# Convolution sequence on one core: weights ahead of x at the head, one t2 half later in the first image, the last image's products reordered

## What is computed

```python
t1 = p1_w * x                          # per channel and row
t2 = x + t1
t4 = relu(x)
t7 = einsum('oc,chw->ohw', p7_w, t4)   # 128 x 128 product
t12 = mean over 5 taps (x - t7 shifted by 3 columns each)
t5 = unfold(x, 3 x 7)                  # 21 neighbours of each pixel
t10 = grouped 1x1 conv of t2 (4 groups, weights p10_w)
t11 = t1 @ t5^T / sqrt(4096)
t13 = t11 @ t10 / sqrt(128 * 21)
out = maximum(t13, t12)
```

## Time and profile before

| | us |
|---|---|
| median of 3 runs | 413.93 |
| lowest and highest run | 413.47, 414.99 |
| the profiled execution | 411.89 |
| its span (first to last instruction) | 409.9 |
| PE busy | 398.8 (97% of the span) |
| DVE busy | 333.6 (81%) |
| ACT busy | 249.4 (61%) |
| POOL busy | 90.0 (22%) |
| DMA queue 1 | 51.4% of 16 engines' span |

### The profile page before, as it was taken

The page is one execution under the profiler, slowest core; times in us unless marked ns, Lnnn a source line. Parts: engine busy times, 40 slices in busy tenths (PEclk is TensorE's granted clock), DMA queues, the critical chain, the costliest instruction groups (busy, mean ns, idle before and its releaser), DMA issues.

```text
span 409.9 us, 12373 instructions
## 1 busy us (share of the span) xinstructions
PE 398.8 (97%) x5126; PEld 250.5 (61%) x5126; DVE 333.6 (81%) x401; ACT 249.4 (61%) x714; POOL 90.0 (22%) x75
## 2 busy tenths in 40 slices
PE   7999999999999999999999999999999999999995
PEld 2333655668655586666888886444766668443663
DVE  6999968899788887888888887888868888786904
ACT  1336728777377755777277771777727775477970
POOL 0582200232023300332003320033202330033300
PEclk9999999999999999999999999999999999999999
DMA  8973263644665447663475635645455542632105
GB/s 295 406 304 109 86 238 116 210 162 158 206 197 176 151 140 221 191 224 104 169 241 201 203 117 187 232 164 164 163 209 187 169 157 80 216 128 95 54 28 206
DMA packets 24104, 72.40 MB, mean 177 GB/s; under 512 B 2800, under 2 KB 3056, under 8 KB 24048
## 3 DMA queue, kind: packets, MB, share of 16 engines
q1 hardware_dynamic: 24048, 71.61, 51.4%
HBM read 54.82 MB, written 16.78 MB: 175 GB/s over the span
## 4 chain that ended last, share of the span: by engine, by line
PE 84%; issue 6%; POOL 3%; DVE 3%; ACT 2%; DMA 2%; DVEq 0%; SPq 0%; ACTq 0%; POOLq 0%
PE ps_y L654 44%; PE ps_y L666 16%; PE ps_p L666 12%; PE ps_t L666 12%; POOL t1T L219 3%; DMA xw<-x_conv 2%; ACT t L314 1%; DVE v_planes L463 0%; DVE v_planes L440 0%; DVE yT L495 0%; DVE v_planes L449 0%; ACT base L259 0%; DVE base L538 0%; ACT relu_pad L272 0%; DVEq L43 0%
## 5 line engine op out<-in xcount | busy, mean ns | idle before, releaser
L654 PE MATMUL ps_y<-v_planes,u_planes 64*64 64x512 f32 x2048 | 257.0, 590 | 0.4
L654 PEld LDWEIGHTS ps_y<-v_planes,u_planes 64*64 64x64 f32 x2048 | 126.1, 133 | 93.6 <-issue 54.7
L219 POOL TENSOR_TENSOR t1T<-t1T,p1T_sb 128x512 f32<-128x512 f32 x64 | 84.1, 1340 | 281.4 <-DVE box L513 152.2
L314 ACT ACTIVATE t<-xn,p_plus 128x64 f32<-128x64 f32 x512 | 128.1, 335 | 0.0
L666 PE MATMUL ps_p<-box,p_fifth 64*64 64x512 f32 x464 | 123.4, 590 | 1.6 <-ACT ps_p L259 1.0
L666 PE MATMUL ps_t<-t,aT 64*64 64x512 f32 x448 | 118.4, 590 | 0.0
L259 ACT ACTIVATE base<-ps_p 128x512 f32<-128x512 f32 x58 | 34.6, 596 | 85.4 <-PE ps_p L666 85.4
L666 PEld LDWEIGHTS ps_y<-t1T,yT 64*64 64x64 f32 x2048 | 58.0, 133 | 8.4 <-DVE yT L495 5.0
L666 PE MATMUL ps_y<-t1T,yT 64*64 64x128 f32 x2048 | 60.7, 270 | 2.0 <-issue 1.2
L666 PEld LDWEIGHTS ps_p<-box,p_fifth 64*64 64x64 f32 x464 | 38.3, 133 | 22.7 <-issue 13.8
L482 DVE SCALAR_TENSOR_TENSOR ps_y<-ps_y,q_sb 128x512 f32<-128x512 f32 x32 | 22.3, 698 | 33.8 <-ACT q_sb L259 33.7
(11 more groups left out here) (42 smaller groups left out, 119.2 us busy)
## 6 DMA issues: line engine op xcount, KB each, us to landing
xw<-x_conv SPq DMA_DIRECT2D x32, 594.0 KB, 5.4
xn<-x_nat SPq DMA_DIRECT2D x32, 512.0 KB, 4.1
t1T<-x_pix SPq DMA_DIRECT2D x32, 512.0 KB, 6.1
out<-base SPq DMA_DIRECT2D x64, 256.0 KB, 2.5
u_planes<-w_tiles SPq DMA_DIRECT2D x4, 384.0 KB, 7.1
p1T_sb<-p1T SPq DMA_DIRECT2D x1, 128.0 KB, 7.5
p_sb<-p7T SPq DMA_DIRECT2D x1, 64.0 KB, 7.3
p_sb<-p SPq DMA_DIRECT2D x1, 32.0 KB, 7.8
```

The costliest lines, as they stand in the source:

```text
L219: nc.gpsimd.tensor_tensor(part, part, p1T_sb[:, e, :].unsqueeze(1).broadcast_to([P, 4, C]), ALU.mult).then_inc(t1_ready, 1)
L314: last = nc.scalar.activation(t2[:, h, W * r:W * (r + 1)], xn[:, f, at:at + W], ACT.Copy, scale=p1_plus[:, 8 * h + r:8 * h + r + 1])
L654: last = nc.tensor.matmul(dst[TILE * pair:TILE * pair + TILE, :], u_planes[rows, u % GROUPS, weights, TILE * k:TILE * k + TILE], v_planes[ ...
```

## The change

It makes no operation faster and leaves out none but part of one zero product. It reorders:

1. **Head.** SP issues the weights of a group ahead of its x for groups 0 and 1; DVE does `weights(0)` ahead of `early_planes(0)` and `weights(1)` ahead of `early_planes(1)`. The three zero products are now one of 256 columns on half of the p7 bank, then t13's bank, then p7's.
2. **First image.** ACT's list loses one t2 half ahead of `relu(1, 1)`; each later `t2_half` stands one place later until image 2's first half, where an extra one catches up.
3. **Around unit 31.** On PE, `outputs_second` of halves b moves behind the rest of unit 31 and `outputs_first` of c. On DVE `turn_y(31)` moves ahead of `max_half(6, 6)` and `box_pairs(7, 3)`.
4. **Last p7 products.** The groups between the blocks of `y_times_t1(7)` move from 16, 24 and 32 blocks to 22, 28 and 32, and each pairs a product of row half 0 with one of row half 1. On ACT `base_half(7, 3)` moves behind `t2_half(7, 3)`, `t2_half(7, 7)` behind `base_half(7, 5)`, and `first_part_of_a(7)` ahead of `base_half(7, 6)`.

```diff
+            load_weights(0)
             load_group(0)
-            load_weights(0)
+            load_weights(1)
             load_group(1)
-            load_weights(1)
...
                     t2_half(0, 4)
-                    t2_half(0, 5)
...
+                late = n == 1
                 relu(n, 1)
                 base_half(n - 1, 6)
                 seed_x(n - 1, 7)
-                t2_half(n - 1, 6)
+                t2_half(n - 1, 6 - late)
...
             seed_x(LAST, 5)
+            t2_half(LAST, 3)
             base_half(LAST, 3)
-            t2_half(LAST, 3)
             seed_x(LAST, 6)
             seed_x(LAST, 7)
-            t2_half(LAST, 4)
             base_half(LAST, 4)
-            for h in range(5, 8):
+            for h in range(4, 7):
                 t2_half(LAST, h)
             base_half(LAST, 5)
+            t2_half(LAST, 7)
+            first_part_of_a(LAST)
             base_half(LAST, 6)
-            first_part_of_a(LAST)
             base_half(LAST, 7)
...
+            weights(0)
             early_planes(0)
-            weights(0)
+            weights(1)
             early_planes(1)
-            weights(1)
             early_planes_rest()
...
             box_last(LAST, 2)
+            turn_y(UNITS - 1)
             max_half(LAST - 1, 6)
             box_pairs(LAST, 3)
-            turn_y(UNITS - 1)
             box_fours(LAST, 3)
...
-            for bank_set in (ps_t13, ps_p7, ps_p7):
-                nc.tensor.matmul(bank_set[:], zeros[:, 0:P], zeros[:, 0:HALF], start=True,
+            for bank_set in (ps_p7[:, 0:HALF // 2], ps_t13, ps_p7):
+                nc.tensor.matmul(bank_set[:], zeros[:, 0:P], zeros[:, 0:bank_set.shape[-1]], start=True,
...
             zero_three(UNITS - 1, False, 0)
-            outputs_second(p_b, t_b, done + 4)
             zero_three(UNITS - 1, False, 1)
             outputs_first(p_c, t_c, done + 5)
+            outputs_second(p_b, t_b, done + 4)
             outputs_second(p_c, t_c, done + 5)
 
-            y_times_t1(LAST, 0, BLOCKS)
-            p7_rows(LAST, 5, 0)
-            p7_rows(LAST, 6, 0).then_inc(item_half, 1)
-            y_times_t1(LAST, BLOCKS, BLOCKS + 8)
+            y_times_t1(LAST, 0, BLOCKS + 6)
+            p7_rows(LAST, 6, 0, True)
+            p7_rows(LAST, 5, 1, True).then_inc(item_half, 1)
+            y_times_t1(LAST, BLOCKS + 6, BLOCKS + 12)
             pe.wait_ge(item_half, done + 6)
-            p7_rows(LAST, 5, 1).then_inc(p7_done, 1)
-            p7_rows(LAST, 7, 0).then_inc(item_half, 1)
-            y_times_t1(LAST, BLOCKS + 8, 2 * BLOCKS)
+            p7_rows(LAST, 5, 0).then_inc(p7_done, 1)
+            p7_rows(LAST, 7, 1, True).then_inc(item_half, 1)
+            y_times_t1(LAST, BLOCKS + 12, 2 * BLOCKS)
             pe.wait_ge(item_half, done + 7)
             p7_rows(LAST, 6, 1).then_inc(p7_done, 1)
-            p7_rows(LAST, 7, 1).then_inc(p7_done, 1)
+            p7_rows(LAST, 7, 0).then_inc(p7_done, 1)
```

More of the change, by code:

```diff
@@ L360, in _ @@
                     t2_half(0, 4)
-                    t2_half(0, 5)
+                elif n == 2:
+                    relu(1, 3)
+                    base_half(1, 2)
+                    seed_x(1, 3)
+                    t2_half(1, 1)
+                    base_half(1, 3)
+                    seed_x(1, 4)
+                    copy_two(8)
+                    t2_half(1, 2)
+                    relu(2, 0)
+                    base_half(1, 4)
+                    seed_x(1, 5)
+                    t2_half(1, 3)
+                    first_part_of_a(1)
+                    t2_half(1, 4)
+                    base_half(1, 5)
+                    seed_x(1, 6)
+                    copy_two(9)
+                    t2_half(1, 5)
                 else:
@@ L388, in _ @@
                 copy_two(u + 2)
-                t2_half(n - 1, 7)
+                t2_half(n - 1, 7 - late)
                 relu(n, 2)
@@ L393, in _ @@
                 seed_x(n, 1)
-                t2_half(n, 0)
+                if late:
+                    t2_half(n - 1, 7)
+                else:
+                    t2_half(n, 0)
                 base_half(n, 1)
@@ L397, in _ @@
                 copy_two(u + 3)
-                t2_half(n, 1)
+                if late:
+                    t2_half(n, 0)
+                else:
+                    t2_half(n, 1)
             seed_x(LAST, 3)
@@ L731, in y_times_t1, with p7_rows @@
                     last.then_inc(a_done, 1)
-            def p7_rows(n, h, half):
-                if half == 0:
+            def p7_rows(n, h, half, first=False):
+                if first:
                     pe.wait_ge(box_steps, BOX_STEPS * (4 * n + h // 2 + 1))
@@ L757, in outputs_first @@
                     if n >= 0:
-                        last = p7_rows(n, h, 0)
+                        last = p7_rows(n, h, 0, True)
                 for n, h in (t,):
```

## The result

The changed kernel takes 408.80 us (median of six runs, 408.13 to 409.64) where the kernel before takes 413.74 (six runs, 412.67 to 414.99). The ratio is 0.989, with a 95% interval of 0.9872 to 0.9907.

A forecast was written before the change was run, and what follows sets the result against it. PE was taken as the bound, busy 398.8 of 409.9 us. Head -0.25, first image -1.31 and tail -1.54 sum to -3.10 us, from the median 413.93 to 410.8 us; range 409.4 to 412.5.

The forecast's parts named there:

- Direction and places: Whole kernel: faster (under 411.86 us, chance 0.68), by PE's idle time at the head, first image and tail.
- Head, -0.25: Kernel start: weights ahead of x and shorter zero products start PE's convolutions earlier; -0.25 us, ends -0.5 and +0.5.
- The fourth rival: Head: PE's clock rises later; some 3 us late +1.2 us (chance 0.09), over 7 us late slower (chance 0.03).
- First image, -1.31: First image: PE's wait for ACT's seed goes whole, as one t2 half leaves the relu's front; ends -1.3 and -0.9.
- DVE didn't take it back: First image, rival: DVE's full stretch from 73.6 doesn't start earlier, so the 1.31 us shrinks towards 0; 412.1 us, chance 0.10.
- Tail, -1.54: Unit 31 to the first t13: y starts 1.05 us earlier and t13 1.54 us earlier; ends 0.5 and 2.3.
- POOL's part: Around unit 31: POOL's last t1 part, 2.36 us beside DVE's pair sum, takes 1.27 once the sum comes later.
- ACT took the place of the removed wait: Tail: ACT's t2 half ahead of the A copy makes it start at 395.85, 1.5 us behind PE.
- (b): First image: moved t2 halves release x's buffers later; quarter 3's load of image 1 stays hidden, 5.5 us against 3.7 to 5.6.
- the seed's 1.3: First image: the 1.31 us PE loses waiting for ACT's seed, forecast to go whole.
- Theory A and C: Formed after the forecast. A: the first trace of before was lucky somewhere. C: loads delay PE's instruction fetches in y_times_t1.

The follow-up runs named there:

- e7: The changed kernel with ACT's first_part_of_a of the last image ahead of its t2 half 7: 406.92 us, ratio 0.9853 against the kernel before.
- e4: The kernel before, with only SP's load of image 2's x, quarter 1, and what queues behind it waiting one more t2 half: 411.77 us, ratio 0.9976.
- e2: The kernel before with the first image's part of the change alone, t2 half 5 one place later: 410.40 us, ratio 0.9933.
- e11: The changed kernel with ACT's A copy ahead of t2 half 7, and x's quarter 1 loaded one t2 half later in images 3 to 7: 404.69 us.
- e3: The kernel before with all of the tail's edits alone (unit 31's order, transposes, p7 groups, ACT's order): 411.71 us, ratio 0.996.

## Why the prediction was right or wrong

- **Direction and places**: right. PE is the bound, and each of the three places gave time.
- **Head, -0.25**: right as a mean. 0.3 was timed, within noise of about 1, and the traces give 0.25 where the rise isn't late. The 0.83 between the two first traces came about because x of unit 1 landed late in the first of before (8.0, in six others of the old order at 7.0 to 7.3) and x of both units early in that of after (5.3 and 8.1; 5.65 and 8.9 were forecast, and in other traces of the new order they were at 5.4 to 6.3 and 8.1 to 9.1). The fourth rival is real: it took place in 2 of 8 traces, at its short form. Its 0.5 us for each us is what the two spacings give (0.85 and 0.43), and a rise 4 us late cost some 1.6 us of PE. No run shows that PE's idle 0.7 us is the cause, nor a rise over 7 us late.
- **First image, -1.31**: the wait went in full, and DVE didn't take it back.
- **Tail, -1.54**: 1.64 by starts, 1.65 timed alone. POOL's part shrank to 1.27 as reasoned (the pair sum beside it had lost a little too, 1.58 against 1.32). Ahead of the result that was a guess from one overlap, in the trace of before; the 48 long parts of the 17 traces show it. ACT took the place of the removed wait: e7 got 1.5 us for that alone.
- **The step that failed** is the passage on the moved t2 halves under "First image" (b). It saw that the transfers behind them would be issued later, asked only whether they would come *too late*, and booked nothing. That they had been coming at a bad time before, into `y_times_t1(1)`, was overlooked. This is a term of -1.0 to -1.5: 1.0 for the load's move alone (e4), 1.5 left of e2's 2.8 beside the seed's 1.3, and 1.25 by the loops (7.05 and five times 8.3 to 9.3 in the six traces with the load at its old place, mean 8.55; 7.30 in both of the changed kernel).
- It could have been suspected. The prediction noted that the profiled execution was 2.04 us below the median and that "nothing in the trace tells of" it. The trace did hold a sign: the same loop took 7.05 to 8.01 us in different images, though all its work is the same. Theory A and C together account for both gaps: 3.8 by starts, less 1.1 lost by longer loops, is 2.7 where the spans show 2.8; and 0.3 (head) + 1.3 + 1.5 (first image) + 1.6 (tail) = 4.7 where the runs show 4.9.
- Without that term the sum was 3.1, and its parts held to 0.1 us. That a sum of starts from one execution came so close to the mean is in part luck, as the head's starts show.

## What to carry to other kernels

When the median of the runs lies well above the one traced execution, look for a place that varies before using that trace's terms: the same loop with unequal durations, or idle time put down to nothing. In this dense loop of short matmuls two fetches of instructions lie 3.5 us apart (e4); a bulk load issued just ahead of the loop held PE back by up to 2.1 us, and issuing that load a few microseconds later cost nothing that could be measured, as its user had slack. And when PE's order is changed around a unit's end, look whether the order of the engine that makes its operands must go with it (2.6 us here).

## What was unexpected of the hardware

- An instruction fetch of 16 KB came 2.9 us into the loop when DMA was 92% busy with data, against 0.4 us when it was idle; PE lost up to 2.1 us for one of them and always went on 1.1 to 1.6 us after its packet. Five loops gained about 0.4 us each from moving loads alone (37.6 to 35.5 us together in the traces of e7 and e11; 2.8 us, with 1.3 of uncertainty, as timed).
- The pause varies: with nearly the same data traffic one execution of the kernel before had none and another 1.3 us.
- Which of POOL and DVE grows went by who started first. Over the 17 traces, where a DVE product with two SBUF inputs started 0.05 us or more ahead of a t1 part and overlapped it (44 parts), the part took 2.2 to 2.4 us; where each such product beside it started over 0.04 us behind it (83 parts), it took 1.26 to 1.29. In the other four they started within 0.03 us of each other, and POOL's part took 2.39 to 2.45. Where a pair sum started 0.2 us ahead of a t1 part (20.5 us, first trace of before) it took its 1.33 and POOL's part 2.22; where it started 0.1 us behind one (20.1 us, e3) it took 2.40 and POOL's part 1.27.
- The granted clock is printed as 1.00 also for the stretch ahead of the first rise, where passes of 512 columns are 0.85 us apart. The rise itself, read from where the spacing halves, wanders: in 15 traces it comes between 5.1 and 7.7 us, in two at 11.3 and 11.4.
